# A hybrid transformer layer on one core: first tile's output projection and first feed-forward units moved across the stage seams

## What is computed

```python
x = x + attention(layernorm(x))      # 32 heads of 32, softmax, output weight attn_ow, bias attn_ob
x = x + ffn(layernorm(x))            # dense = x @ weight.T + bias, kept only where two selections hold
x = x + bind_attention(layernorm(x)) # 4 heads of 256, causal, sigmoid in place of softmax
x = x + ffn(layernorm(x))            # the same weights and selections again

# ffn's selections
dots = softmax(x @ centroids.T / 0.1)
hits = dots > 0.01                   # tokens x 64 clusters
out = where(any(hits, 1)[:, None] & any(hits, 0)[assignments][None, :], dense, 0)
```

## Time and profile before

| What | us |
|---|---|
| median of 3 runs | 3279.01 |
| lowest and highest | 3276.21, 3280.91 |
| the profiled execution's own time | 3280.28 |
| its span in the trace | 3278.5 |
| TensorE busy | 3153.2 |
| VectorE busy | 2264.4 |
| GpSimd busy | 1937.3 |
| ScalarE busy | 1744.8 |

### The profile page before, as it was taken

How to read it: one execution, slowest core, us unless ns; L and a number is a source line. 1 busy time by engine, 2 the same in 40 slices (tenths; PEclk the granted TensorE clock), 3 DMA queues, 4 the chain that set the end, 5 groups by cost and what they waited for, 6 DMA issues and landing times. The chain is left out here.

```text
span 3278.5 us, 62409 instructions
## 1 busy us (share of the span) xinstructions
PE 3153.2 (96%) x24128; PEld 1718.0 (52%) x24128; DVE 2264.4 (69%) x3904; ACT 1744.8 (53%) x2125; POOL 1937.3 (59%) x2062
## 2 busy tenths in 40 slices
PE   5999999999999999999999899998999999999999
PEld 2455555555555555555444455555466666665344
DVE  7777777777777777777878587776466666653622
ACT  4667777777777777767677422222245555552000
POOL 3577777777777777777677422221466666650522
PEclk9999999999999999999999799999999999999999
DMA  6122222222222222222344644453222333224642
GB/s 222 45 67 63 78 63 74 63 77 66 72 66 72 66 72 67 71 64 68 98 129 123 196 161 161 160 163 117 103 84 103 110 107 112 97 84 156 244 154 96
DMA packets 286055, 344.11 MB, mean 105 GB/s; under 512 B 92225, under 2 KB 215105, under 8 KB 285762
## 3 DMA queue, kind: packets, MB, share of 16 engines
q1 hardware_dynamic: 281090, 323.33, 31.3%
q10 hardware_dynamic: 4608, 16.78, 1.3%
q0 software_dynamic: 64, 0.01, 0.0%
HBM read 200.95 MB, written 138.55 MB: 104 GB/s over the span
## 5 line engine op out<-in xcount | busy, mean ns | idle before, releaser
L727 DVE TENSOR_REDUCE nmax<-ring_ps 128x1 f32<-128x512 f32 x1024 | 676.4, 685 | 387.0 <-PE ring_ps L486 384.3
L887 POOL TENSOR_TENSOR elo<-e,ehi 128x1024 f16<-128x1024 f32 x256 | 669.2, 2614 | 358.8 <-ACT ehi L629 358.8
L623 ACT ACTIVATE e<-st_ps,exp_scale 128x1024 f32<-128x1024 f32 x512 | 570.7, 1115 | 378.9 <-PE st_ps L496 315.6
L537 PE MATMUL proj_ps<-xnT,arena 128*128 128x512 f16 x3024 | 738.8, 380 | 23.2 <-DVE arena L829 23.2
L629 ACT ACTIVATE ehi<-st_ps,exp_scale 128x1024 f16<-128x1024 f32 x512 | 568.5, 1110 | 0.0
L1642 PE MATMUL f_ps<-wT,fxT 128*128 128x512 f16 x1920 | 435.7, 380 | 2.9 <-DMA fxT<-xT_scratch 2.9
L537 PEld LDWEIGHTS proj_ps<-xnT,arena 128*128 128x128 f16 x3024 | 267.8, 97 | 300.3 <-DVE arena L829 23.6
L486 PE MATMUL ring_ps<-ks,qs 96*128 96x512 f16 x1024 | 398.8, 390 | 20.2 <-DVE nmax L727 19.2
L496 PE MATMUL st_ps<-qs,ks 98*128 98x512 f16 x1024 | 393.9, 385 | 11.0 <-ACT ehi L629 10.9
L513 PEld LDWEIGHTS ctx_ps<-v_sb,ehi 128*128 128x128 f16 x4096 | 313.0, 98 | 155.1 <-DVE sums L754 39.2
L513 PE MATMUL ctx_ps<-v_sb,ehi 128*128 128x65 f16 x4096 | 372.7, 192 | 12.5 <-DVE sums L754 11.2
(11 more groups left out here) (233 smaller groups left out, 4695.8 us busy)
## 6 DMA issues: line engine op xcount, KB each, us to landing
qk_scratch<-qk_hl SPq DMA_DIRECT2D x128, 256.0 KB, 2.3
fxT<-xT_scratch SPq DMA_DIRECT2D x64, 512.0 KB, 3.5
qs<-qk_scratch SPq DMA_DIRECT2D x192, 128.0 KB, 2.6
ks<-qk_scratch SPq DMA_DIRECT2D x192, 128.0 KB, 2.9
arena<-x_scratch SPq DMA_DIRECT2D x48, 512.0 KB, 4.4
ctx_scratch<-ctx SPq DMA_DIRECT2D x64, 256.0 KB, 3.2
xb<-in_L_attn_a_x_dram SPq DMA_DIRECT2D x32, 512.0 KB, 4.4
x_scratch<-xb SPq DMA_DIRECT2D x32, 512.0 KB, 2.6
```

Of the source, the lines that this page charges most:

```text
L537: mm = pe.matmul(bank(u), wqk(g, qk, wp, c), xnT[:, b % 2, xp, c, :], start=(n == 0), stop=(n == 23))
L623: nc.scalar.activation(e32[:, half], st_ps[:, half], ACT.Exp, scale=exp_scale[:, 0:1]).then_inc(e32_done, 1)
L727: dve.tensor_reduce(nmax[:, h % 2, c:c + 1], ring_ps[:, ring_max(h, c) % 2, :], AX.X, ALU.max, negate=True).then_inc(ring_free, 1)
L887: nc.gpsimd.tensor_tensor(elo[:, h % 2, 2:4, :], e32[:, 1], ehi[:, h % 2, 2:4, :], ALU.subtract).then_inc(elo_pool, 1)
```

## The change

At the first seam: the contexts of tiles 0 and 1 are loaded in slots 243 and 244 (`CX_LOAD`) and turned in the last slots, half a tile each at (246, 2), (247, 1), (252, 3) and (253, 1), through `proj_ps`. `BIAS` moves from 251 to 248; the bias units go in pieces of three matmuls over eight quarters each, from (248, 0) and from (250, 1), and each piece waits for its own part of the output weight. `leave_bias` moves to (250, 0) and (252, 1). Tile 0's two projection units are issued in pieces of three from slot 254 on, into `ring_ps`, which now outlives the stage and is the second stage's `o_ps`. The second stage starts with the two residuals of tile 0 and has no turn of tiles 0 and 1, no load of x and no bias sum for tile 0 (GpSimd does that sum at (253, 3)).

At the second seam: in step 28 the turned tiles 0 and 1 are loaded back into `fxT_first`, a part of the arena. The first two feed-forward units run in the second stage's steps 32 to 34 (`ffn_early`, pieces of 14, 10 and 24 matmuls), and stay in the banks that are the third stage's `f_ps`. The third stage begins with unit 2, and does not load tiles 0 and 1 again.

The core of the diff, first seam:

```diff
-                BIAS = REST + 2
+                CX_LOAD = WO_LOAD + 2
+                BIAS = WO_LOAD + 7
+                cx_turn_at = {(BIAS - 2, 2): (0, 0), (BIAS - 1, 1): (0, 1), (BIAS + 4, 3): (1, 0), (BIAS + 5, 1): (1, 1)}
+                bias_leave_at = {(BIAS + 2, 0): 0, (BIAS + 4, 1): 1}
+                cx_dst = (xnT[:, 0, :, :, P:2 * P], cT_second)
                 for half in range(2):
-                    for q in range(4):
-                        fills.setdefault((BIAS + 2 * half, q), []).append((("B", half), 6 * q, 6 * q + 6))
+                    for q in range(8):
+                        fills.setdefault(at(4 * BIAS + 9 * half + q), []).append((("B", half), 3 * q, 3 * q + 3))
+                        fills.setdefault(at(4 * (TOT - 2) + 8 * half + q), []).append((("O", half), 3 * q, 3 * q + 3))
...
+                            t = s - CX_LOAD
+                            if 0 <= t < 2:
+                                sp.wait_ge(wo_out, 16 * C)
+                                sp.wait_ge(ctx_out[0], 16 * GH)
+                                sp.wait_ge(ctx_out[1], 16 * GH)
+                                sp.dma_start(xt[:, t].rearrange("p (g d) -> p g d", d=P),
+                                             ctx_t[0, :, t].rearrange("g p d -> p g d")).then_inc(cx_in, 16)
+                            if t == 2:
+                                sp.wait_ge(proj_full, place["QK", GROUPS - 5, 1] + 1)
+                                sp.dma_start(x0b, x_t[0, 0]).then_inc(x0b_in, 16)
...
                             if a == 0 and half == 0:
-                                pe.wait_ge(proj_free, len(order))
+                                pe.wait_ge(cx_lo, 2)
                                 pe.wait_ge(bvx_hi, 1)
                                 pe.wait_ge(bvx_lo, 1)
-                                pe.wait_ge(wo_in, 16 * C)
                             elif a == 0:
                                 pe.wait_ge(ob_done, 1)
                             for n in range(a, z):
                                 c, (xp, wp) = n // 3, ((0, 0), (0, 1), (1, 0))[n % 3]
+                                if half == 0 and n % 3 == 0:
+                                    pe.wait_ge(wo_in[c], 16)
...
+                        def project_first(u, a, z):
+                            half = u[1]
+                            if a == 0:
+                                pe.wait_ge(cx_lo, 2)
+                                pe.wait_ge(ring_free, T * TOT)
+                            for n in range(a, z):
+                                c, (xp, wp) = n // 3, ((0, 0), (0, 1), (1, 0))[n % 3]
+                                mm = pe.matmul(ring_ps[:, half, :], cx_dst[0][:, xp, c, :], wo_part(c)[:, wp, S * half:S * half + S],
+                                               start=(n == 0), stop=(n == 23))
...
+                                if c == 3 and s == BIAS + 5:
+                                    pool.wait_ge(x0b_in, 16)
+                                    pool.wait_ge(ob_done, 2)
+                                    nc.gpsimd.tensor_tensor(x0b, x0b, obias, ALU.add).then_inc(x0b_done, 1)
```

and the second seam:

```diff
+                            if k == W_FIRST + 2 * C:
+                                sp.wait_ge(w_turned, 2 * C)
+                                for t in range(2):
+                                    sp.wait_ge(xT_out[t], 16)
+                                    sp.dma_start(fxT_first[:, t], xT1_d[t]).then_inc(first_in, 16)
...
-                        turn_context(0)
+                        def ffn_early(half, a, z):
+                            if a == 0:
+                                pe.wait_ge(x1_done, 2 * (NT - 1) + half + 1)
+                                pe.wait_ge(first_in, 32)
+                                pe.wait_ge(w_lo, 2 * C)
+                            for i in range(a, z):
+                                c, (xp, wp) = i // 3, ((0, 0), (0, 1), (1, 0))[i % 3]
+                                pe.matmul(o_ps[:, half, :], fxT_first[:, 0, xp, c, :], wT[:, wp, c, 512 * half:512 * half + 512],
+                                          start=(i == 0), stop=(i == 23))
+
                         for k in STEPS:
+                            if k == NT:
+                                ffn_early(0, 0, 14)
+                            if k == NT + 1:
+                                ffn_early(0, 14, 24)
+                            if k == NT + 2:
+                                ffn_early(1, 0, 24)
                             project(k, 0)
...
-                        lo_context(0)
+                        residual(0, 0)
+                        residual(0, 1)
                         for k in STEPS:
...
-                        biases(0)
                         for k in STEPS:
...
-                            wait(sp, f_full, 8 * b + 2 * t - 2)
+                            if T * b + t < 2:
+                                return
+                            if T * b + t >= 4:
+                                sp.wait_ge(f_full, 8 * b + 2 * t - 2 - EARLY)
...
-                            if not 0 <= b < B + 2:
+                            if not 0 <= b < B + 2 or 8 * b + u < EARLY:
                                 return
```

More of the change, by code:

```diff
@@ L568, in bias_unit, with turn_context @@
                                 mm.then_inc(bias_full, 1)
+                        def turn_context(t, half):
+                            if half == 0:
+                                pe.wait_ge(cx_in, 16 * t + 16)
+                            if t:
+                                pe.wait_ge(ob_done, 2)
+                            else:
+                                pe.wait_ge(proj_free, len(order))
+                            wait(pe, cx_lo, 2 * t + half)
+                            for c in range(4):
+                                h0 = P * (4 * half + c)
+                                mm = pe.transpose(proj_ps[:, P * c:P * c + P], xt[:, t, h0:h0 + P], ident[:])
+                            mm.then_inc(cx_full, 1)
+                        def project_first(u, a, z):
[7 more added lines that the diff above has]
+                                               start=(n == 0), stop=(n == 23))
+                            if z == 24:
+                                mm.then_inc(first_full, 1)
                         def turn_first(t):
@@ L1119, in turn_context @@
                         def turn_context(n):
-                            if not tile(n):
+                            if not tile(n) or n < TURNED:
                                 return
-                            wait(pe, ct_in[n % 3], 16 * (n // 3 + 1 if n % 3 else n // 3))
-                            src = ct[:, n % 3] if n else ct0
+                            pe.wait_ge(ct_in[n % 3], 16 * ((n + 1) // 3))
+                            src = ct[:, n % 3]
                             wait(pe, w_lo, min(n - 1 - W_FIRST, 2 * C))
                             for half in range(2):
-                                wait(pe, cT_lo, 2 * (n - 1) + half + 1)
+                                wait(pe, cT_lo, 2 * (n - 1) + half + 1 - 2 * TURNED)
                                 for c in range(4):
@@ L1132, in project @@
                         def project(n, half):
-                            if not tile(n):
+                            if not tile(n) or n < PROJECTED:
                                 return
-                            pe.wait_ge(cT_lo, 2 * n + 2)
+                            wait(pe, cT_lo, 2 * n + 2 - 2 * TURNED)
+                            src = cT[:, n % 2] if n >= TURNED else cT_second
                             wait(pe, x1_done, 2 * (n - 1) + half + 1)
@@ L1193, in hi_context @@
                         def hi_context(n):
-                            if not tile(n):
+                            if not tile(n) or n < TURNED:
                                 return
-                            wait(act, o_full, 2 * (n - 2) + 2)
+                            wait(act, o_full, 2 * (n - 2) + 2 - 2 * PROJECTED)
                             for half in range(2):
-                                act.wait_ge(cT_full, 2 * n + half + 1)
+                                act.wait_ge(cT_full, 2 * n + half + 1 - 2 * TURNED)
                                 nc.scalar.activation(cT[:, n % 2, 0, 4 * half:4 * half + 4, :],
@@ L1284, in residual @@
                             cols = slice(512 * half, 512 * half + 512)
-                            dve.wait_ge(xb_done, n + 1)
-                            dve.wait_ge(o_full, 2 * n + half + 1)
+                            wait(dve, xb_done, n)
+                            wait(dve, o_full, 2 * (n - PROJECTED) + half + 1)
+                            src = xb[:, n % 4] if n else x0b
                             dve.scalar_tensor_tensor(out=xb[:, n % 4, cols], in0=o_ps[:, half, :], scalar=inv_o[:, 0:1],
-                                                     in1=xb[:, n % 4, cols], op0=ALU.mult, op1=ALU.add).then_inc(x1_done, 1)
```

(6 more changed lines are left out.)

87 lines of the change are left out of this document (55 added, 32 removed).

## The result

The changed kernel takes 3287.28 us (median of 14 runs, 3281.60 to 3294.31) against 3280.86 us of the kernel before on the same chip (14 runs). The ratio is 1.002, 95% interval 1.0012 to 1.0028. The forecast was 3269.5 us, and its range ended at 3279.

A forecast was written before the change was run, and what follows sets the result against it. TensorE, busy for 96% of the span, was taken to bound the kernel. Last slots +5, second stage's head -3.6, its end -1.2 and third stage's head -9.7 sum to -9.5: 3269.5 us from 3279.0, range 3260 to 3279.

The forecast's parts named there:

- the term of the last slots: Last head slots before the second stage: added work and late loads cost 5 us, range 0 to 9.
- late operands: Last head slots: last output weight piece and row bias land after they are now needed; 3.2 us lost.
- VectorE is nearly full here, so I take 0.5 us for each slot: Slots 246, 247, 252 and 253: copy and subtraction of turned contexts cost 0.5 us a slot.
- so it fits: Slot 253: GpSimd's late bias sum of 2.34 us fits, since GpSimd was busy 6.24 of 10.5 us.
- The added TensorE work: Last slots: 48 projection matmuls, 16 transposes and spread bias chunks; with the turns' copies and subtractions, +1.8 us.
- the tail behind slot 255: Slots 255 to 257: one chunk adds 0.65 us at most, covered by GpSimd's last work; taken as 0.
- last rival: Third stage does not follow: its head waits for x or GpSimd's sums, only first seam counts; 3280 us, chance 0.05.
- The second stage's head: Start of second stage: GpSimd free 5 us earlier, 1.4 us lost to low clock; net -3.6, range -7 to 0.
- The end of the second stage: Second stage's last steps: 48 feed-forward matmuls keep the clock up, store chain ends earlier; -1.2 us, range -2 to +1.
- The third stage's head: Start of third stage: unit 2 starts 12.1 us earlier, less 2.3 for low clock; net -9.7, range -12 to -7.
- the last slots eat most of it: Rival, last head slots: late operands and low clock together cost +9 or more; about 3276 us, chance 0.19.
- dense work at half clock: Rival, slots holding fills: each us of low clock costs half a us; 42 us of it give 3287, chance 0.07.

The follow-up runs named there:

- spreading: Changed kernel with early loads and GpSimd's sum moved to VectorE, plus VectorE's subtraction of each turned half two quarters behind the transposes (one in the last case): 3274.56 us, ratio 0.998.

## Why the prediction was wrong

**The step that failed is the term of the last slots**: "+5", measured +17.7, beyond its range of 0 to +9. It had mis-sized the turns' part (the waits they bring in VectorE's order) most of all, and the late operands' part after that. Its parts:

- "VectorE is nearly full here, so I take 0.5 us for each slot": 2.0 in all, measured 9.4. I had priced the subtraction by its own length and left out that it waits for ScalarE's copy, which is written at the same place but behind exponentials of 1.1 us; the four waits, 6.1 us, were a cost of the order, and spreading gave 5.25 us back. The rest would fit the subtractions' own 2.8 us and VectorE's collisions with GpSimd; no run separates these. Of the 9.4 us, 6.4 lie in slots 253 and 254; the other 3 lie where executions scatter.
- "so it fits", GpSimd's late sum at nothing: nothing to be seen in the changed kernel (15.4 us with it, 15.7 without), but by luck. The reason was wrong: GpSimd had time, but while it sums, VectorE's two-input operations stand still. The turns hid this; with them out the sum costs 7 us.
- Late operands, 3.2: the waits forecast are there (0.95 and 3.25 us). Their price is 3.4 us by the run with early loads and 5.6 by the ratios. The 7.6 us that the turns and the matmuls leave over lie in slots 247 to 252, ahead of the sum, where executions scatter. Behind the wait comes a clock of 0.50, which the term had put elsewhere.
- The added TensorE work, 1.8 less the turns' 2.0, so nothing: measured 0.8, near enough. But the tail behind slot 255, taken at 0, grew by 1.3 us (15.0 to 16.3), and slots 247 to 254 shrank by 0.4.

Two slips in its sums change nothing: 9.19 + 0.38 + 8.39 is 18.0 and 7.12 + 0.38 + 6.73 is 14.2, where 17.8 and 14.1 stand, and the last rival's terms give 3279, not 3280.

**The second stage's head**: GpSimd was to be free 5 us earlier; the normalisation starts 23.2 us behind the stage's start instead of 28.3. With both gaps, 15.3 us in all where 14.1 to 17.8 was taken, right in mechanism and size: tile 2's unit starts 5.1 us nearer where 5 was taken. The 1.4 us taken off for a low clock came to 0.5: the turn took 2.0 us against 1.7 before, the unit 6.5 against 6.3. The run without the reduction shows that a further 7.6 us hang on it. A wait of 4.0 us for tile 2's context was not foreseen.

**The end of the second stage**: the 24 matmuls ended at 2306.75 and the third stage began at 2307.83. Before, it began 3.5 us behind the queue's last issue (2292.26 to 2295.74); by that, the queue would have allowed 2307.3. So TensorE ended the stage, 0.5 us later; the forecast had the queue last. From tile 2's unit to the third stage it took 407.2 us against 406.6: +0.6 where -1.2 was taken. A miss of 1.8 us that the head made up. The second seam alone, in its one profiled execution, took 1.2 us longer from second to third stage, too, where 1 shorter was expected.

**The third stage's head**: -10.5 where -9.7 was taken; right, and shown alone by the run with the second seam only.

**The rivals**: "the last slots eat most of it" named the right place with too small a price. The one on the slower side, dense work at half clock, gave the right time, 3287, by a mechanism that did not occur: the stretch it rested on was at 1.00, and by the clocks of the windows (0.88 and 0.89 after, 0.78 and 1.00 before) slots 247 to 254 had some 14 us of low clock both before and after, where it needed 42. It is not to be counted as right.

**Is the first seam's idea wrong?** With its loads, sum, turns and reduction mended it is at 3269.77 us, the second seam alone at 3269.07, each against its own chip's before at a ratio of 0.996 and with intervals that cover each other. So it gains nothing that can be told apart. In the profiled executions it has 6 us more in the slots and 8 less from second to third stage than before; what would remain, 2 us, is less than either interval's width. The version to keep is the second seam alone, 10.4 us faster than before with the smaller edit.

## What to carry to other kernels

When work moves into slots that another engine paces, price it on that engine, and price its place in the order: an operation whose operand comes from an engine that is itself full waits for that engine's queue, and a gap of two quarters between producer and consumer was worth more than the operation. Look also at which operand is now due earlier than its load, and at who must be free at the same time. Remove suspected causes together once, and not only one by one: the sum and the turns, each taken out alone, left slots 253 and 254 as long as they were in the changed kernel, and both together gave back 6 us. And compare first the stretch ahead of an edit, where two executions should agree: here they differed by up to 4.8 us, and a gain of 1.4 us turned out to lie there.

## What the runs showed of the hardware

- While GpSimd runs an operation that began first, a VectorE operation with two inputs outside `ring_ps` and its like stands still until it ends, however small: 1.68 to 2.04 us beside a 128x1024 sum or subtraction where 0.16 is the shortest, 2.75 to 2.97 where 1.22 is usual. With GpSimd's copy of 1.04 us it is 0.82. The other way round, in the changed kernel 194 of GpSimd's 128x1024 subtractions begin inside VectorE's: they take 2.9 us (median) instead of 2.13, while each of the 220 VectorE subtractions that found GpSimd idle at its start kept its 1.22. The Trainium skill (SBUF — State Buffer, Who interferes with whom) states an exclusive lock of a shared port pair for the whole instruction, and that it is issue order that decides who waits; the trace agrees.
- A partition reduction at the head of the second stage had 6.7 to 9.7 us without visible work ahead of its 0.38 us and 6.8 to 8.4 behind it, in the profiles of all kernels that have it there, in step 0 and in step 1 alike. In the changed kernel's trace both gaps open with the same two records of GpSimd's sequencer, under the reduction's line ahead of it and under the next operation's line behind it (its x4 counts both reductions of the stage). What they load or change, and whether they are the cause of the gaps, was not tested.

```profile
L1522 POOLq MODIFY_POOL_CONFIG  x2: 6/6/6, 1879.8 to 1879.8; - x2
...
L1513 POOLq MODIFY_POOL_CONFIG  x4: 83/83/83, 1887.5 to 2016.7; - x4
```
